# One-expert layers of an eight-expert transformer step: rows fetched by token instead of sent to slots, results stored by slot and fetched by token, norms cut finer

## The chip, the cores and the metric

One core of one Trainium2 chip runs the whole program. The metric is the device time in microseconds of one execution. Engines are TensorE (PE), VectorE (DVE), ScalarE (ACT), GpSimd (POOL) and SyncE (SP), which here only issues DMAs. Each has its own instruction stream; they meet at semaphores only.

## The reference

`x` is 4 x 1024 tokens of 128 numbers. Six residual steps are applied, each to the layer norm of `x`:

```
x = x + 0.5 * L0_ffn(norm(x))     # 8 experts, each token goes to one
x = x + L0_attn(norm(x))          # gated linear attention, a recurrence over the tokens, done in chunks
x = x + 0.5 * L0_ffn(norm(x))
x = x + 0.5 * L1_ffn(norm(x))     # 8 experts, each token goes to its best two
x = x + L1_attn(norm(x))          # gated attention unit
x = x + 0.5 * L1_ffn(norm(x))

def L0_ffn(x):                    # T = 4096 tokens, E = 8, cap = T // E
    probs = softmax(x @ Wg)
    # each expert takes its cap best tokens; a token goes to its best expert
    # among those that took it, or to its best expert if none did
    tok2exp = ...
    out[t] = probs[t, tok2exp[t]] * gelu(x[t] @ W1[e]) @ W2[e]
```

The matrices of `L0_ffn` are 128 x 256 and 256 x 128, those of `L1_ffn` 128 x 512 and 512 x 128.

## The kernel before

The 4096 tokens are 32 tiles of 128 rows; `x` and its norm `xn` stay in SBUF. The layers are called moe0, gla (the recurrent attention), moe2, moe3, gau (the gated unit) and moe6. moe0 and moe2 give each token one expert (K = 1), moe3 and moe6 two (K = 2).

**Experts.** `moe_vector` routes on VectorE: softmax, a search of 15 steps for the eight thresholds, and a slot number for each token so that the tokens of one expert stand together in tiles. Slots for K = 1 fill 39 tiles, 20 pairs. From the slot numbers TensorE inverts the list by one-hot matmuls into `token`, the token of each slot. The slot numbers are known at L865, `token` at L897 (K = 1, where L895 and L896 give empty slots rows of their own) or L900 (K = 2).

For K = 1 the rows travel so. `fill_sync` (SP) fills the DRAM array `xslots` with rows of `xn`. `slots_pool` (GpSimd) issues 32 indirect DMAs, L1080, one a tile of tokens, that send each row of `xn` to its slot. When all have landed, `slots_sync` (SP) fetches slots in order, four tiles an issue (L1021), into a ring of eight pairs. In the loop `finish` (VectorE, L942) copies the result of a pair from PSUM into a ring of four, `ysb`, once the scatter of four pairs earlier has landed; `slots_pool` sends the result by 39 indirect DMAs (L1089) to the row of its token. When all have landed, SP reads the results in token order into `yhome`.

For K = 2 `moe_pool` (GpSimd) gathers the rows from DRAM by `token` (L1065), one indirect DMA a tile, four pairs ahead of TensorE's transposes (`AHEAD`); `moe_sync` (SP) stores the results in slot order (L1040), and behind the loop `moe_bring` gathers them by slot number, one indirect DMA a tile (L1106), into a ring of 16 tiles.

**The loop over pairs.** TensorE runs in a fixed order: the transposes of pair t+3 (`turn`, L598 for K = 1, L603 for K = 2), the up-projection of t+2 (`up`, L619 to L621), the down-projection of t (`down`, L640 to L643). ScalarE takes the gelu (L694, L695), VectorE splits the turned rows (L921, L923) and the hidden ones (L931) into high and low bf16 halves, and copies the result.

**Combination and norm.** `combine` (VectorE, L983) adds gate times result to `x`, four tiles at a time, then the statistics of the next norm (L352). `moments` turns the statistics of a group of tiles into scale and shift, by some 20 small operations each of which waits for the one before (L321 to L332, and `newton`, L296 to L301). ScalarE then writes the norms (L403), TensorE turns four tiles a block (L379), VectorE (L367) or ScalarE (L413) copies them. Norm ln1 (ahead of gla) has groups of 8 and 24 tiles, and `halves`, a bf16 split of the turned norm (L370 on VectorE, L410 on ScalarE); ln2 (ahead of moe2) groups of 8, 8 and 16; ln3 (ahead of moe3) of 8 and 24. In `ln_tensor` the work on a turned block (router logits L391 or queries L1138) follows two blocks behind the turning. `moe_rows_pool` (GpSimd) splits the norm into halves for moe3's rows.

**gla.** 32 chunks of 128 tokens in four batches. TensorE in `stage2` multiplies an update of the state (L1175) once VectorE has subtracted (L1340) and scaled (L1343) the state before; ScalarE copies (L1231, L1232) two products, and behind them the chunk's output and its sum of squares (L1245, L1246). VectorE's scans (L1313) and reciprocals (L1319) serve four chunks each. After the last chunk `gla_vector` adds the result to `x` (L1380) and takes the statistics.

**Weights.** moe3's and moe6's weights are split into bf16 halves during moe0: the high ones on ScalarE, the low ones on VectorE (`split_low`, L258, eight operations of 128 x 1024) just ahead of moe0's loop.

## Time and profile before

| | us |
|---|---|
| median of 3 runs | 1283.04 (1280.93 to 1285.11) |
| the profiled execution | 1278.25 |
| its span, first to last instruction | 1276.1 |
| PE busy | 672.3 (53%) |
| DVE busy | 738.6 (58%) |
| ACT busy | 489.5 (38%) |
| POOL busy | 553.1 (43%) |

How to read it. Busy times are of one profiled execution; a difference is made against its own 1278.25, and the median is 4.8 above that. In a timeline a row gives the start in us, the duration (of several merged operations with xN), engine, line and operation, what it writes and reads, and in brackets how long the engine had been idle and what ended that. The duration of an indirect DMA on POOL is that of its issue, not of the transfer; the transfer's landing is seen at whoever waits for it. `<-remote` says that the releaser is nothing that the profile lists, such as a DMA's landing; `<-issue` that the engine waited for nothing that shows. The chain of work goes back from the last instruction, at each step to what released it.

### The profile page before, as it was taken

The numbers are of one execution on the slowest core, as the hardware profiler recorded it, in microseconds if no ns is written. First come the engines' busy times: TensorE is split into PE (matmuls) and PEld (weight loads), VectorE is DVE, ScalarE is ACT, GpSimd is POOL, SyncE is SP. The second block draws the span as 40 slices with busy tenths as digits, with TensorE's granted clock in tenths as the row PEclk, the third lists the DMA queues.
The fourth block names the chain that finished last, engine by engine and source line by source line (L and its number), as shares of the span: only waits on it lengthen the run. The fifth ranks groups of instructions, "written<-read, shape, count | busy, mean of one in ns | idle before, by whom it ended". The sixth has DMA issues, their size and how long they took to land.

```text
span 1276.1 us, 20751 instructions
## 1 busy us (share of the span) xinstructions
PE 672.3 (53%) x5982; PEld 544.7 (43%) x5983; DVE 738.6 (58%) x2301; ACT 489.5 (38%) x1079; POOL 553.1 (43%) x538
## 2 busy tenths in 40 slices
PE   4210582466646111870659999127777448999100
PEld 4210451245635000550648888014445337889100
DVE  6682354767884850547354556339985764556222
ACT  5300232544435000331507788126555206788000
POOL 2117563044440045561236666654311126663575
PEclk9999996679875555885558999668878659999655
DMA  9401313000000002213102334111000102335232
GB/s 294 120 8 46 92 57 92 1 1 0 0 3 1 1 27 80 72 43 90 50 23 68 76 82 67 49 43 34 25 17 9 34 15 67 77 81 71 61 82 68
DMA packets 86769, 67.78 MB, mean 53 GB/s; under 512 B 10522, under 2 KB 78362, under 8 KB 86706
## 3 DMA queue, kind: packets, MB, share of 16 engines
q1 hardware_dynamic: 72978, 38.99, 10.7%
q0 software_dynamic: 13728, 28.02, 9.4%
q8 instruction: 31, 0.51, 0.2%
q14 instruction: 32, 0.26, 0.1%
HBM read 38.53 MB, written 28.44 MB: 52 GB/s over the span
## 4 chain that ended last, share of the span: by engine, by line
PE 36%; DVE 26%; POOL 13%; issue 12%; ACT 6%; DMA 3%; another core or an unknown queue 3%; DVEq 0%; POOLq 0%; ACTq 0%; SPq 0%
POOL rt L1106 6%; POOL xslots L1080 5%; PE bank L619 4%; PE bank L640 4%; PE bank L621 3%; PE bank L643 3%; PE bank L620 3%; DVE rt L800 3%; PE bank L641 3%; PE bank L391 2%; DVE stats L352 2%; DVE x L983 2%; PE bank L603 1%; DVE turned L931 1%
## 5 line engine op out<-in xcount | busy, mean ns | idle before, releaser
L1065 POOL DMA_INDIRECT turned<-xrows_moe,token x156 | 168.7, 1081 | 144.1 <-DVE token L900 60.7
L702 ACT ACTIVATE turned<-bank,b1T 128x256 f32<-128x256 f32 x312 | 122.4, 475 | 111.4 <-PE bank L621 93.8
L1106 POOL DMA_INDIRECT rt<-y_moe,slot_i x128 | 122.7, 959 | 87.7 <-issue 37.2
L931 DVE TENSOR_TENSOR turned<-turned 128x1024 bf16<-128x1024 f32 (+1 forms) x118 | 125.3, 1062 | 34.9 <-ACT turned L706 18.5
L640 PE MATMUL bank<-w2h,turned 128*128 x780 | 141.0, 224 | 4.6 <-DVE turned L931 2.3
L641 PE MATMUL bank<-w2h,turned 128*128 x780 | 141.0, 224 | 1.0 <-issue 1.0
L619 PE MATMUL bank<-rt,w1h 128*128 128x256 bf16 (+1 forms) x468 | 126.3, 270 | 26.3 <-issue 11.1
L1080 POOL DMA_INDIRECT xslots<-xn,slot_i x64 | 69.4, 1084 | 163.1 <-DVE slot_i L865 144.2
L942 DVE COPY arena<-bank 128x256 f32<-128x256 f32 x118 | 49.8, 422 | 141.2 <-remote 89.9
L620 PE MATMUL bank<-rt,w1h 128*128 128x256 bf16 (+1 forms) x468 | 125.5, 268 | 0.0
L621 PE MATMUL bank<-rt,w1l 128*128 128x256 bf16 (+1 forms) x468 | 125.2, 268 | 0.0
L694 ACT ACTIVATE turned<-bank 128x512 f32<-128x512 f32 x40 | 23.9, 598 | 263.5 <-PE bank L621 229.1
L643 PE MATMUL bank<-w2l,turned 128*128 x780 | 122.9, 224 | 0.5 <-issue 0.4
L1089 POOL DMA_INDIRECT y_moe<-arena,token x78 | 77.8, 998 | 68.9 <-DVE arena L942 50.3
L379 PE MATMUL bank<-consts,xn 128*128 128x128 f32 x128 | 33.5, 412 | 115.7 <-ACT xn L403 115.6
L983 DVE SCALAR_TENSOR_TENSOR x<-rt,small,x 128x128 f32<-128x128 f32 x128 | 40.9, 349 | 77.2 <-DMA rt<-y_moe,slot_i 72.6
L640 PEld LDWEIGHTS bank<-w2h,turned 128*128 128x128 bf16 x780 | 76.8, 99 | 16.8 <-issue 10.8
L403 ACT ACTIVATE xn<-x,nwt 128x128 f32<-128x128 f32 x128 | 52.1, 482 | 82.3 <-DVE credit L360 81.9
L706 ACT ACTIVATE turned<-turned 128x1024 bf16<-128x1024 f32 x78 | 82.4, 1057 | 2.5
L641 PEld LDWEIGHTS bank<-w2h,turned 128*128 128x128 bf16 x780 | 77.8, 100 | 1.4 <-issue 0.9
L379 PEld LDWEIGHTS bank<-consts,xn 128*128 128x128 f32 x128 | 24.2, 226 | 124.0 <-ACT xn L403 90.0
L619 PEld LDWEIGHTS bank<-rt,w1h 128*128 x468 | 47.2, 101 | 51.8 <-issue 41.7
(302 smaller groups left out, 1835.4 us busy)
## 6 DMA issues: line engine op xcount, KB each, us to landing
y_moe<-arena SPq DMA_DIRECT2D x78, 128.0 KB
turned<-xslots SPq DMA_DIRECT2D x18, 256.0 KB
arena<-y_moe SPq DMA_DIRECT2D x16, 256.0 KB, 4.7
xslots<-xn SPq DMA_DIRECT2D x5, 512.0 KB, 6.0
turned<-xrows_moe,token POOLq DMA_INDIRECT x156
x<-in_x SPq DMA_DIRECT2D x4, 512.0 KB, 5.9
arena<-in_w SPq DMA_DIRECT2D x1, 2048.0 KB, 9.4
turned<-in_w SPq DMA_DIRECT2D x8, 256.0 KB, 4.4
```

The costliest lines, as they stand in the source:

```text
L619: nc.tensor.matmul(o, wh, xh_t, start=True, stop=False)
L620: nc.tensor.matmul(o, wh, xl_t, start=False, stop=False)
L621: last = nc.tensor.matmul(o, wl, xh_t, start=False, stop=True)
L640: nc.tensor.matmul(y[j], hh[j], wh, start=(u + j == 0 and not s["bias"]), stop=False)
L641: nc.tensor.matmul(y[j], hl[j], wh, start=False, stop=False)
L643: last = nc.tensor.matmul(y[j], hh[j], wl, start=False, stop=(u == FC - 1 and j == js[-1]))
L702: last = nc.scalar.activation(s["h32"][:, k % 2, o], bank[1 + 2 * (k % 2) + u // 2][:, W * (u % 2):W * (u % 2) + W], ACT.Gelu, bias=b1T[:, ...
L706: nc.scalar.activation(s["hh"][:, k % 4], s["h32"][:, k % 2], ACT.Copy).then_inc(s["act"], 1)
L931: nc.vector.tensor_tensor(s["hl16"][:, k % 4], s["h32"][:, r], s["hh"][:, k % 4], ALU.subtract)\
L1065: nc.gpsimd.indirect_dma_start(out=s["xs"][:, 2 * (t % BODY) + j], out_offset=None, in_=s["xdram"], in_offset=bass.IndirectOffsetOnAxis(ap ...
L1080: nc.gpsimd.indirect_dma_start(out=s["xdram"], out_offset=bass.IndirectOffsetOnAxis(ap=slot_i[:, 0, t:t + 1], axis=0), in_=xn[:, t, :], in ...
L1106: nc.gpsimd.indirect_dma_start(out=ytok[:, at % TOK], out_offset=None, in_=s["ydram"], in_offset=bass.IndirectOffsetOnAxis(ap=slot_i[:, k, ...
```

## The change

Seven parts.

1. For K = 1 rows and results travel as for K = 2: SP stores `xn` in token order (`rows_sync`), `moe_pool` gathers the rows by `token` four pairs ahead, `moe_sync` stores results by slot, `moe_bring_all` gathers them by slot number behind the loop. `fill_sync`, `slots_sync`, `slots_pool` and the rows of empty slots go.
2. `combine_all`: with K = 1 the statistics of a tile follow its addition at once, and after each addition three steps of the moments of the group before (`moments_by_steps`, a generator) are written out; the copies and splits of turned blocks follow two groups behind.
3. The groups: ln1 8, 8, 8, 4, 4; ln2 8, 8, 8, 8; ln3 8, 8, 8, 4, 4. In `gla_vector` the moments are written between additions and statistics.
4. The split of moe3's rows goes from GpSimd to ScalarE (high) and VectorE (low, `ln_rows`).
5. `ln_tensor`: logits and queries follow one block behind the turning.
6. `split_low` is halved: four operations ahead of moe0's loop, four behind it; the second weights are staged in `xn` and loaded once the rows are stored.
7. gla: the update matmul waits for the subtraction alone, the copy of the two products for a semaphore of its own, and the two copies are one; the sums of squares are copied once a batch.

```diff
         def load_w2(sp):
-            sp.wait_ge(pr["w0l"], 2)
+            sp.wait_ge(*ln0.at("turned", NS))
+            sp.wait_ge(*moe0.at("xrow", 16 * B))
...
+        def moments_by_steps(dve, s, g):
...
+            dve.wait_ge(*s.at("stat", b))
+            done(nc.vector.tensor_tensor(one(0), st(1), st(4), ALU.add))
+            yield
...
+        def some_steps(chain):
+            for _ in range(3):
+                next(chain, None)
...
+        def ln_halves(dve, s, blocks, chain=iter(())):
+            def copy(i):
...
+                dve.wait_ge(*s.at("turned", i + 1))
+                nc.vector.tensor_copy(xnT[:, o], bank[i % 2][:]).then_inc(s["copied"], 1)
+                next(chain, None)
+            def low(i):
...
+                dve.wait_ge(*s.at("copied", i + 1))
+                dve.wait_ge(*s.at("high", i + 1))
                 nc.vector.tensor_tensor(xl[:, o], xnT[:, o], xh[:, o], ALU.subtract).then_inc(s["low"], 1)
+                next(chain, None)
+            copy(blocks[0])
+            for i in blocks[1:]:
+                copy(i)
+                low(i - 1)
+            low(blocks[-1])
+        def ln_rows(dve, s, blocks, chain=iter(())):
+            for i in blocks:
+                tiles = slice(TPS * i, TPS * (i + 1))
+                dve.wait_ge(*s.at("high", i + 1))
+                nc.vector.tensor_tensor(xhl[:, tiles, P:2 * P], s["dst"][:, tiles], xhl[:, tiles, 0:P], ALU.subtract)\
+                    .then_inc(s["low"], 1)
+                next(chain, None)
...
-                if i >= 2:
-                    after(i - 2)
-            after(NS - 2)
+                if i >= 1:
+                    after(i - 1)
             return after(NS - 1)
...
+                if s["rows"]:
+                    tiles = slice(TPS * i, TPS * (i + 1))
+                    act.wait_ge(*s.at("norm", TPS * (i + 1)))
+                    nc.scalar.activation(xhl[:, tiles, 0:P], s["dst"][:, tiles], ACT.Identity).then_inc(s["high"], 1)
...
-                if K == 1:
-                    i = k % BODY // 2
-                    pe.wait_ge(fetched[i], FETCHED[s["layer"]][i] + 16 * (c + k // BODY) + 16)
-                else:
-                    pe.wait_ge(gathered[k % BODY], GATHERED[k % BODY][s["index"]] + 32 * (c + k // BODY) + 16 * len(js))
+                pe.wait_ge(gathered[k % BODY], GATHERED[k % BODY][s["index"]] + 32 * (c + k // BODY) + 16 * len(js))
...
-                if K == 1:
-                    dve.wait_ge(scattered[k % YRING], SCATTERED[k % YRING][s["index"]] + 32 * turns)
-                else:
-                    dve.wait_ge(ystored[k % YRING], YSTORED[k % YRING][s["index"]] + 16 * turns)
+                dve.wait_ge(ystored[k % YRING], YSTORED[k % YRING][s["index"]] + 16 * turns)
...
+                    if K == 1:
+                        some_steps(chain)
+                        dve.wait_ge(*s.at("comb", QUAD * quad + i + 1))
+                        next_stats([t])
...
+            for quad in range(groups[0][1] // QUAD):
+                combine(dve, s, quad, count)
+            for g in range(1, last + 1):
+                chain = moments_by_steps(dve, next_ln, g - 1)
+                for quad in range(groups[g][0] // QUAD, groups[g][1] // QUAD):
+                    combine(dve, s, quad, count, chain)
+                finish_steps(chain)
+                if 2 <= g < last:
+                    blocks(*groups[g - 2])
+            chain = moments_by_steps(dve, next_ln, last)
+            blocks(groups[last - 2][0], groups[last - 1][0], chain)
+            finish_steps(chain)
+            blocks(groups[last - 1][0], NT)
...
                     pe.wait_ge(gl["act1"], n + 3)
-                    pe.wait_ge(gl["state"], n + 1)
+                    pe.wait_ge(gl["dve"], n + 1)
                     nc.tensor.matmul(DS[:, 0:P], ga["kt"][:, i % 2], ga["v"][:, i % 2], start=True, stop=True)\
                         .then_inc(gl["update"], 1)
...
+                    pe.wait_ge(gl["state"], n + 1)
                     nc.tensor.matmul(O[:, 0:P], state, ga["qT"][:, tok], start=False, stop=True).then_inc(gl["st2"], 1)
...
-        ln1 = layernorm(x, xn, [8, 24], halves=True)
-        ln2 = layernorm(x, xn, [8, 8, 16])
+        ln1 = layernorm(x, xn, [8, 8, 8, 4, 4], halves=True)
+        ln2 = layernorm(x, xn, [8, 8, 8, 8])
...
-        ln3 = layernorm(x, xn, [8, 24])
+        ln3 = layernorm(x, xn, [8, 8, 8, 4, 4], halves="rows")
...
-            slots_pool(pool, moe0, gau_pool)
+            moe_pool(pool, moe0, gau_pool)
+            moe_bring_all(pool, moe0)
             gla_pool(pool)
             rows_pool(pool)
-            slots_pool(pool, moe2)
+            moe_pool(pool, moe2)
+            moe_bring_all(pool, moe2)
             gau_select(pool)
-            moe_rows_pool(pool, moe3)
...
-            moe_vector(dve, moe0, split_low)
+            moe_vector(dve, moe0, lambda dve: split_low(dve, 0), lambda dve: split_low(dve, 1))
```

## Rows read from the trace of the kernel before

**Rows 1.** The page, part 4: shares of the chain by line.
```profile
POOL rt L1106 6%; POOL xslots L1080 5%; PE bank L619 4%; PE bank L640 4%; PE bank L621 3%; PE bank L643 3%; PE bank L620 3%; DVE rt L800 3%; PE bank L641 3%; PE bank L391 2%; DVE stats L352 2%; DVE x L983 2%; PE bank L603 1%; DVE turned L931 1%
```
**Rows 2.** Timeline of POOL, first, one middle and last of moe0's scatters.
```profile
88.39 1.91 POOL L1080 DMA_INDIRECT xslots<-xn,slot_i  x1 [52.27 <-DVE slot_i L865]
...
100.69 1.96 POOL L1080 DMA_INDIRECT xslots<-xn,slot_i  x1 [0.30 <-issue]
...
133.20 0.97 POOL L1080 DMA_INDIRECT xslots<-xn,slot_i  x1 [0.30 <-issue]
```
**Rows 3.** Chain in moe0, timeline of PE in moe2: first up-projection of each.
```profile
140.23 0.28 PE bank L619
...
507.82 0.29 PE L619 MATMUL bank<-rt,w1h 128*128 128x128 bf16 x1 [0.77 <-DVE rt L923]
```
**Rows 4.** Timeline of DVE ahead of moe0's loop, and of moe2's.
```profile
94.36 0.23 DVE L895 TENSOR_SCALAR rt<-iotas,consts 128x40 f32<-128x40 f16 x1
...
96.05 4.63 DVE L258 TENSOR_TENSOR w1l<-arena,w1h 128x1024 bf16<-128x1024 f32 x4
...
139.12 0.42 DVE L921 CAST rt<-bank 128x256 bf16<-128x256 f32 x1 [33.91 <-PE bank L598]
...
465.25 0.23 DVE L895 TENSOR_SCALAR rt<-iotas,consts 128x40 f32<-128x40 f16 x1
```
**Rows 5.** Waits of DVE over the span, and its last result copies in moe0.
```profile
DVE arena L942 <- remote: 89.9, 49, 4.0
...
206.05 0.76 DVE L942 COPY arena<-bank 128x256 f32<-128x256 f32 x2 [4.02 <-remote]
```
**Rows 6.** Timelines around ln1 and ln3: DVE moments (first, last), ACT, PE, DVE.
```profile
219.06 0.17 DVE L321 TENSOR_TENSOR nwt<-stats 128x8 f32<-128x8 f32 x1
...
222.19 0.17 DVE L332 TENSOR_TENSOR nwt<-nwt 128x8 f32<-128x8 f32 x1
...
238.38 1.63 ACT L403 ACTIVATE xn<-x,nwt 128x128 f32<-128x128 f32 x4
...
257.87 1.85 PE L1152 MATMUL bank<-turned,wkT_s 128*128 128x512 f32 x2 [0.89 <-ACT arena L1211]
...
627.10 0.42 DVE L771 TENSOR_REDUCE small<-bank 128x32 f32<-128x256 f32 x1 [18.98 <-PE bank L391]
```
**Rows 7.** Timelines of DVE, POOL and PE where moe3's loop starts.
```profile
653.10 0.24 DVE L900 TENSOR_SCALAR token<-bank 128x78 int32<-128x78 f32 x1 [0.87 <-PE bank L562]
...
654.14 1.27 POOL L1065 DMA_INDIRECT turned<-xrows_moe,token  x1 [31.50 <-DVE token L900]
...
661.81 0.39 PE L619 MATMUL bank<-rt,w1h 128*128 128x256 bf16 x1 [0.33 <-issue]
```
**Rows 8.** PE's transposes in moe2's loop; a window (PE, PEld, DVE, ACT, POOL, clock, DMA).
```profile
521.46 0.41 PE L598 MATMUL bank<-consts,turned 128*128 128x128 f32 x2
...
524.08 0.41 PE L598 MATMUL bank<-consts,turned 128*128 128x128 f32 x2
...
503.00:510.00 7.00, 3.26 (x23) 2.69 (x24) 1.60 (x4) 0.49 (x1) 0.00 (x0) 0.50 0.65 187
```
**Rows 9.** Timeline of DVE behind moe6's loop: last copy, first and last use.
```profile
1185.71 0.42 DVE L942 COPY arena<-bank 128x256 f32<-128x256 f32 x1 [1.57 <-PE bank L643]
...
1191.41 0.35 DVE L983 SCALAR_TENSOR_TENSOR x<-rt,small,x 128x128 f32<-128x128 f32 x1 [5.27 <-DMA rt<-y_moe,slot_i]
...
1270.68 0.35 DVE L983 SCALAR_TENSOR_TENSOR x<-rt,small,x 128x128 f32<-128x128 f32 x1 [0.90 <-DMA rt<-y_moe,slot_i]
```
**Rows 10.** Timeline of PE in gla: the update matmul and what it waited for.
```profile
314.12 0.46 PE L1175 MATMUL bank<-arena 128*128 128x128 f32 x2 [1.97 <-DVE arena L1343]
```
**Rows 11.** Timeline of DVE: moe2's router takes its first reduction.
```profile
409.87 0.42 DVE L771 TENSOR_REDUCE small<-bank 128x32 f32<-128x256 f32 x1 [14.39 <-PE bank L391]
```
**Rows 12.** Timeline of DVE in gau's first steps, while POOL gathers (L1106).
```profile
830.20 0.17 DVE L1745 TENSOR_TENSOR nwt<-stats 128x4 f32<-128x4 f32 x1 [3.72 <-issue]
...
833.70 0.17 DVE L1750 TENSOR_SCALAR nwt<-nwt 128x4 f32<-128x4 f32 x1 [3.18 <-remote]
```

268 lines of the change are left out of this document (124 added, 144 removed).

## The prediction

> **What bounds the kernel now.** I read the page's chain of work first [rows 1]: no engine is the bound throughout, and the two dearest lines of the chain are not arithmetic but GpSimd's indirect DMAs, L1106 (results fetched by token for the two-expert layers) with 6% and L1080 (rows sent to their slots for the one-expert layers) with 5%. Then I cut the span at the stages by the timelines of single engines. In the first one-expert layer VectorE knows the slots at 88 us, GpSimd issues 32 scatters one behind the other, the last at 133.20 [rows 2], and TensorE's first up-projection starts at 140.23 [rows 3]; VectorE has stood 33.91 us before it [rows 4]. Then 20 pairs of tiles run until 206.4 [rows 5], and the combination, the norm and the queries until the keys' matmul at 257.87 [rows 6]. The second one-expert layer is the same 370 us later: first up-projection 507.82, next router's first reduction 627.10 [rows 3, 6]. Inside the loops the longest wait is VectorE's copy of results, 89.9 us in 49 waits for something outside the engines [rows 5]: a ring buffer that comes free only when the result scatter of four pairs earlier has landed. So three things bound these layers: 32 exposed issues ahead of the loop, a scatter in the loop, and a norm of 24 tiles that can't start before its last tile.
>
> **Issues are exchanged, not removed.** Per one-expert layer GpSimd had 32 scatters ahead of the loop and 39 in it; now it has 39 gathers in the loop and 32 behind it. What was exposed ahead of the loop is exposed behind it. The gain must come from what can run beside the 32, from a faster loop, and from fewer landings in series. I therefore sum each layer from end to end, from the moment the token list is known.
>
> **First layer.** The token write takes the place of the operation at 94.36 [rows 4], since what stood before it is dropped. In the two-expert layer, which has the same gathers, the token write at 653.10, the first gather at 654.14 and the first up-projection at 661.81 give 1.0 and 7.7 us [rows 7] (up-projection 0 waits for the rows of pair 1, four issues). Four instead of eight of the weight splits now run on VectorE just there; beside them an issue took 1.96 instead of 0.97 us [rows 2]. Up to three of the four issues are hit; I take 1.5 us, between 0 and 3. 94.4 + 1.0 + 7.7 + 1.5 = 104.6 for the first up-projection, instead of 140.2.
> The Trainium skill, page "SBUF — State Buffer", section "Who interferes with whom", says that a tensor_tensor without a two-port mode should not hold up the writing of descriptors; by it these 1.5 us, and 1 more below, would be 0. The issue at 100.69 beside the split says otherwise.
>
> The loop: two transposes in a row of TensorE start at 521.46 and 524.08 with nothing missing between them, so TensorE needs 2.62 us a pair at full clock [rows 8]. GpSimd's two issues need 2 x (0.97 + 0.30) = 2.54 us [rows 2]. The result store moves to SP, and its ring no longer waits for GpSimd. The two rates are nearly equal and coupled by a ring four pairs deep: at least 20 x 2.62 = 52.4, and I add 5.6 for filling, draining and jolts: 58.0, against 66.2 now. Bounds: 55 (perfect) and 66 (as now). At the low clock, with which the second layer starts (0.50 [rows 8]), TensorE is a little over 3 us a pair at first; 1 us there. Last result copy 162.6.
>
> Behind it: in the last layer the last result copy starts at 1185.71, the first use of a gathered tile at 1191.41, the 64th at 1270.68 [rows 9]: 5.7 us, and 79.27 / 63 = 1.258 us a tile. For 32 tiles 39.0 us. The other four weight splits (4.6 us [rows 4]) fit into the 5.7 but slow two issues: 1 us. First use 169.3, last tile landed 208.3.
>
> Beside the gathers VectorE now does combination, statistics, three steps of the moments a tile and the norm's copies. One tile: 0.27 + 0.2 for the two operations and some 0.43 for three dependent steps (20 steps take 3.1 us when bare [rows 6]), 0.9 us. This alone would keep up with 1.258. But each pair of blocks adds two copies and two subtractions (four of 0.69, 2.8 us, by what each takes at 128 x 512) and a hole: ScalarE writes the next block's four norms (1.63 [rows 6]) between the two halves VectorE waits for. I take 4.5 us a pair of blocks. Followed through in order, from the first use: groups 0 and 1 are paced by the gathers until 20; group 2 ends at 30, its blocks at 34.3; group 3 at 39, blocks at 43.9; the last four tiles at 48.6; then blocks 4 and 5 with the last steps, 56, where the last tile landed at 39. Then norms 1.6, turning 1.1, a copy, two query matmuls and their activations, some 7.5: 64. So the keys' matmul at 169.3 + 64 = 233.3 against 257.87: **24.6 us gained**. A check: today the way from the last statistics' end, 233.5, to the keys is 24.4 us with nothing hidden; put behind the last landing it would be 39 + 24.4 = 63.4. By my count the finer norm thus gives nothing that VectorE's fixed order doesn't take back.
>
> **Second layer.** Token write 465.25 [rows 4], nothing else on VectorE: 465.3 + 1.0 + 7.7 = 474.0. Loop 59 (with the clock), then 5.7: 538.7. The tail is the same with cheaper blocks (3.5, since ScalarE copies and VectorE only subtracts) and norms, turning and two blocks of logits, 5.8, at the end: 58.5. 597.2 against 627.10: **29.9 gained**. GpSimd's split of rows for the next layer goes to ScalarE and VectorE; I count it in these blocks. Its store to memory lies below the routing, over 25 us long.
>
> **The recurrent layer.** TensorE's update matmul now waits for the difference, not for the scaled state, so it runs beside the 0.35 us scaling; where it waited 1.97 us for L1343 it now waits 0.4 less [rows 10]. Its 0.46 us also stood on the chain. ScalarE merges two copies and leaves out seven of eight small ones. VectorE's scans and reciprocals, some 10 of 24 us a batch, stay. 32 chunks, a third of them waiting so: 32 x 0.46 / 3 = 5. Bounds 0 (VectorE bound throughout) and 12. **5 us.** The norm behind it: four groups of eight with moments between the additions, last group 8 instead of 16 tiles. Today four blocks of TensorE follow the last moments, the router's reduction waiting 14.39 us to 409.87 [rows 11]. New: the last moments end at about 393.6, only 1 us earlier, but the blocks 4 and 5 are turned before; two blocks remain: 402.8. **7 us**, between 4 and 8. The first norm turns logits one block earlier; TensorE is the bound there, 0 within 1 us either way. The second weights' load moves behind the rows' store on SP, into the norm's buffer; its cover is the routing, until 88 us [rows 2], and if it were late ScalarE would only start its splits later beside the gathers: 0. The row stores that open the one-expert layers lie there too. SP's 20 result stores a layer stand behind nothing else on its queue. Routing, both two-expert layers and the gating layer: 0.
>
> **Sum.** 24.6 + 29.9 + 5 + 7 = 66.5. The profiled execution took 1278.25 (2.1 around its span of 1276.1): 1211.8. The median of the runs stands 4.8 above it, 1283.04: **1217 us**, the forecast.
>
> **Rivals.**
> B. VectorE keeps up. If ScalarE's halves come early and steps hide beside other work, the last norms start soon after the last tile: 39 + 8 for the last steps + 7.5 = 54.5 to the keys, 39 + 7.2 + 5.8 = 52 to the router. That is 9.5 and 6.5 us less, and 3 more each with the loops at 55: 22, about 1195. For it: the bare step's 0.2 us is latency, its issue takes under 0.1. Against it: four engines in fixed orders must meet in each block.
> C. Loops no faster than now, and stalls. VectorE stood 3.72 us before L1745, then twice 3.2 more, and ran its next steps at some 0.7 instead of 0.2 us, while GpSimd gathered [rows 12]; about 16 us in all, in code that runs once. The new combination is such code beside such gathers. With loops at 66 (+8 each) and 8 us of stall a layer left on the path: 66.5 - 32 = 34.5, about 1249; one of the two alone gives 1233. For it: [rows 12], and that the loop's rate has two makers of equal speed; against it: the quads before and after show no such stall.
> The Trainium skill, page "Runtime: NRT & Kernel Launch", section "Instruction fetch mechanics", says that passing to the next block of instructions is mostly hidden in straight code. If the waits of [rows 12] are that, the rows differ from it by 3 us each; what they are no row tells.
> D. Slower than before. The same stall in every quad of the new combination: there are 16 in the two layers, and from 66.5 / 16 = 4.2 us a quad on the gain is gone. Stalls of 3.72 and some slow steps, 6 us a quad, would give 1217 + 96 = 1313. Against it: the gating layer has eight quads and stood so in one or two.
> That the change doesn't do what it says, in its finer norms, is the check above: it costs nothing against the forecast.
>
> **Chances.** Forecast 0.50, B 0.25, C 0.20, D 0.05, of which 0.02 at about its point of balance. The range takes in B and C: 1194 to 1249. Faster by over 0.3% (about what a measurement of this kernel can tell from no change) 0.95, within 0.02, slower 0.03.
>
> **What the profile of after would show.** GpSimd's first gather of the first layer at 95 to 96, first up-projection at 104 to 106 (right if within 2 us); pairs at 2.7 to 2.9 us, and the copy's waits for something outside near 0; 32 gathers 1.26 us apart; VectorE's last combination some 9 us behind the last landing; keys near 233, the router's reduction after the second one-expert layer near 561 (627.1 less 66.5). It is wrong if pairs take over 3.1 us (C), if VectorE waits for a landing at the last tile (B), or if VectorE shows repeated idle times of 3 us in the combination (C, D).

## The result, and the profile after

| | before | after |
|---|---|---|
| median, us | 1283.48 (1280.93 to 1285.11, 4 runs) | 1260.88 (1259.44 to 1265.05, 4 runs) |
| ratio after / before | | 0.983 (95%: 0.980 to 0.985) |
| the profiled execution / its span | 1278.25 / 1276.1 | 1261.09 / 1257.9 |

The change gained 22.6 us by the medians (of four runs each here, of three in the table ahead of the prediction) and 17.2 between the two profiled executions, where the forecast was 66.5. The time is 44 us above the forecast and outside the range. The stations of the prediction, in the changed kernel (timelines of GpSimd, TensorE and VectorE; columns as in the rows ahead of the prediction):

```profile
93.32 1.11 POOL L1104 DMA_INDIRECT turned<-xrows_moe,token  x1 [57.12 <-DVE token L956]
...
101.95 0.29 PE L684 MATMUL bank<-rt,w1h 128*128 128x128 bf16 x1 [0.47 <-issue]
...
169.08 0.42 DVE L994 COPY arena<-bank 128x256 f32<-128x256 f32 x1 [0.43 <-PE bank L708]
...
175.40 0.35 DVE L1033 SCALAR_TENSOR_TENSOR x<-rt,small,x 128x128 f32<-128x128 f32 x1 [1.35 <-DMA rt<-y_moe,slot_i]
...
253.94 1.10 PE L1171 MATMUL bank<-turned,wkT_s 128*128 128x512 f32 x2 [0.89 <-ACT arena L1231]
...
361.07 2.19 DVE L1401 SCALAR_TENSOR_TENSOR x<-xn,nwt,x 128x128 f32<-128x128 f32 x8
...
395.13 0.42 DVE L836 TENSOR_REDUCE small<-bank 128x32 f32<-128x256 f32 x1 [9.33 <-PE bank L472]
...
458.71 0.29 PE L684 MATMUL bank<-rt,w1h 128*128 128x128 bf16 x1 [0.25 <-issue]
...
526.54 0.42 DVE L994 COPY arena<-bank 128x256 f32<-128x256 f32 x1 [0.32 <-PE bank L708]
...
532.55 0.35 DVE L1033 SCALAR_TENSOR_TENSOR x<-rt,small,x 128x128 f32<-128x128 f32 x1 [5.58 <-DMA rt<-y_moe,slot_i]
...
606.55 0.42 DVE L836 TENSOR_REDUCE small<-bank 128x32 f32<-128x256 f32 x1 [0.64 <-PE bank L472]
```

Set beside [rows 3, 6, 11]: the first up-projection comes 38.3 us earlier, but gla's keys only 3.9; the router behind gla 14.7; the router behind moe2 20.6. So nearly all the gain of the front was given back behind it. That the 32 gathers now stand behind the loop was forecast; two stretches of each one-expert layer took longer than that. The first is the loop: first up-projection to last result copy is 67.1 us in moe0 and 67.8 in moe2, where 58 and 59 were forecast and the kernel before took 66.2 and 63.5. The second is the tail, from the first addition to the keys, 78.5 us, and in moe2 to the router, 74.0, where 64 and 58.5 were forecast.

What each place shows. Where the loop begins, ScalarE and VectorE stand 7 to 9 us (their timelines), and over the run the result copy waits as before for something outside the engines (waits of VectorE: total, times, longest):

```profile
113.85 0.60 ACT L759 ACTIVATE turned<-bank 128x512 f32<-128x512 f32 x1 [8.94 <-remote]
...
114.00 0.42 DVE L976 CAST rt<-bank 128x256 bf16<-128x256 f32 x1 [7.57 <-remote]
```

```profile
DVE arena L994 <- remote: 94.6, 65, 3.0
...
DVE arena L994 <- PE bank L708: 37.1, 38, 2.0
```

This total is of all four expert layers, as the 89.9 us of [rows 5] are. In moe0's and moe2's loops alone the copy stood 13.0 and 14.8 us so (9 and 11 times), and 66.9 us in moe3's and moe6's.

In the tail VectorE keeps up with the gathers until 193 us; then this (timeline of VectorE):

```profile
193.12 0.16 DVE L402 TENSOR_TENSOR nwt<-nwt 128x8 f32<-128x8 f32 x1
194.59 0.29 DVE L352 BATCH_NORM_STATS2 stats<-x 128x6 f32<-128x128 f32 x1 [1.31 <-issue]
...
197.41 0.29 DVE L352 BATCH_NORM_STATS2 stats<-x 128x6 f32<-128x128 f32 x1 [2.28 <-remote]
197.62 0.34 DVE L1033 SCALAR_TENSOR_TENSOR x<-rt,small,x 128x128 f32<-128x128 f32 x1
...
205.14 0.17 DVE L376 TENSOR_SCALAR nwt<-nwt 128x8 f32<-128x8 f32 x1 [2.99 <-remote]
205.22 0.16 DVE L378 SCALAR_TENSOR_TENSOR nwt<-nwt 128x8 f32<-128x8 f32 x1
205.30 0.22 DVE L380 TENSOR_SCALAR nwt<-nwt 128x8 f32<-128x8 f32 x1
207.94 0.29 DVE L352 BATCH_NORM_STATS2 stats<-x 128x6 f32<-128x128 f32 x1 [2.42 <-remote]
208.15 0.34 DVE L1033 SCALAR_TENSOR_TENSOR x<-rt,small,x 128x128 f32<-128x128 f32 x1
211.45 0.17 DVE L383 TENSOR_TENSOR nwt<-nwt 128x8 f32<-128x8 f32 x1 [2.96 <-issue]
215.64 0.17 DVE L386 TENSOR_SCALAR nwt<-nwt 128x8 int32<-128x8 int32 x1 [4.02 <-remote]
```

Read it by what each instruction waits for. L352, L376, L383 and L386 (and L369, at 199.51, not shown) wait for a semaphore that VectorE itself has just incremented, and start 1.3 to 4.0 us late. L378 and L380 wait for nothing, and L1033 waits for a tile that has long landed: they start at once. Eight such starts from 193 to 216 are 19.3 us (1.31 + 2.28 + 1.55 + 1.76 + 2.99 + 2.42 + 2.96 + 4.02). They end with the gathers: the last long one begins at 211.62, when the last gather is issued (211.57), and two of 0.5 to 0.6 us follow. moe2's tail shows eight more between 553 and 573, 0.9 to 3.7 us each, 18.3 us together. I call them late starts.

### The profile page after: what moved, and what is told of

It reads as the page before. It is cut to its first block, busy times and chain, and to the rows that moved or that the text cites. A ratio compares the mean times of both kernels' runs of the same rounds, so it can differ in the third digit from the quotient of the medians.

```text
span 1257.9 us, 20818 instructions
## 1 busy us (share of the span) xinstructions
PE 679.3 (54%) x5975; PEld 545.5 (43%) x5983; DVE 759.4 (60%) x2446; ACT 489.1 (39%) x1027; POOL 530.8 (42%) x530
## 4 chain that ended last, share of the span: by engine, by line
PE 35%; DVE 21%; issue 12%; POOL 9%; ACT 6%; another core or an unknown queue 4%; DMA 2%; POOLq 0%; DVEq 0%; ACTq 0%
POOL rt L1124 8%; PE bank L684 4%; PE bank L705 4%; PE bank L686 3%; PE bank L685 3%; PE bank L706 3%; PE bank L708 3%; DVE rt L865 2%; PE bank L668 1%; ACT xn L484 1%; DVE x L1033 1%; DVE stats L352 1%; DVE arena L1339 1%; POOL turned L1104 1%
## 5 line engine op out<-in xcount | busy, mean ns | idle before, releaser
L1104 POOL DMA_INDIRECT turned<-xrows_moe,token x234 | 243.4, 1040 | 373.4 <-DVE token L956 243.2
L1124 POOL DMA_INDIRECT rt<-y_moe,slot_i x192 | 183.5, 956 | 139.4 <-DMA y_moe<-arena 57.6
L994 DVE COPY arena<-bank 128x256 f32<-128x256 f32 x118 | 50.0, 424 | 131.9 <-remote 94.6
L1033 DVE SCALAR_TENSOR_TENSOR x<-rt,small,x 128x128 f32<-128x128 f32 x192 | 63.0, 348 | 96.2 <-DMA rt<-y_moe,slot_i 91.9
L708 PEld LDWEIGHTS bank<-w2l,turned 128*128 128x128 bf16 x780 | 64.1, 99 | 4.4 <-issue 3.9
L686 PEld LDWEIGHTS bank<-rt,w1l 128*128 x468 | 48.1, 103 | 5.6 <-issue 0.6
```

The source lines that it names most:

```text
L686: last = nc.tensor.matmul(o, wl, xh_t, start=False, stop=True)
L708: last = nc.tensor.matmul(y[j], hh[j], wl, start=False, stop=(u == FC - 1 and j == js[-1]))
L1033: nc.vector.scalar_tensor_tensor(x[:, t, :], ytok[:, at % TOK], gates[k][:, t:t + 1], x[:, t, :], ALU.mult, ALU.add).then_inc(s["comb" if ...
L1104: nc.gpsimd.indirect_dma_start(out=s["xs"][:, 2 * (t % BODY) + j], out_offset=None, in_=s["xdram"], in_offset=bass.IndirectOffsetOnAxis(ap ...
L1124: nc.gpsimd.indirect_dma_start(out=ytok[:, at % TOK], out_offset=None, in_=s["ydram"], in_offset=bass.IndirectOffsetOnAxis(ap=slot_i[:, k, ...
```

## The experiments

"Beside it" is the kernel before on the same chip; a ratio is against it, with its 95% interval. The eighteen kernels ran in five sets on five chips. The chip turned out to matter more than most edits, so I take the sets in the order in which they ran.

**Transport by SP in the tail.** The results are then those of other tokens, and only time and waits are read.

```diff
+            for at, t in enumerate(s["order"]):
+                if at >= 6:
+                    sp.wait_ge(*s.at("comb", at - 5))
+                sp.dma_start(ytok[:, at % TOK], s["ydram"][P * t:P * (t + 1)]).then_inc(direct[at % 6], 16)
...
-            moe_bring_all(pool, moe0)
```

> Edit: in moe0 and moe2 the 32 tiles of results behind the loop are fetched by SP with plain DMAs in slot order instead of by GpSimd's indirect gathers by slot number (results are then those of other tokens: the order by token is left out). Same bytes, same VectorE code. Theory S (VectorE gets its code late while GpSimd's gathers are in flight): the idle times of 1.3 to 4.0 us in VectorE's combination (22 us in moe0, 20 in moe2) are gone, each below 0.6 us; with the tiles arriving faster too, the keys' matmul of gla at 253.9 comes 20 to 35 us earlier. Rival W (the code itself, its waits from step to step or for ScalarE and TensorE, makes these times): they stay, some 20 us in each layer, wherever the tiles come from.

1189.64 us, beside it 1277.78. From the first addition at 172.46 the keys come in 49.9 us:

```profile
222.37 1.10 PE L1183 MATMUL bank<-turned,wkT_s 128*128 128x512 f32 x2 [0.89 <-ACT arena L1243]
```

No late start is left in the tails; the long waits of VectorE in moe0's are six for ScalarE, 5.5 us, and one of 2.1 for TensorE, and the changed kernel has these too (5.5 and 2.0). The same VectorE code without GpSimd's gathers beside it is not late. W is out. (The loops still gather, and keep their 65.9 and 66.2 us.)

**More code, a larger ring, a closer lead.** Three kernels on the same chip.

```diff
+            for i in range(64 * s["index"], 64 * s["index"] + 64):
+                nc.vector.memset(padding[:, i:i + 1], 0.0)
```

> Edit: 64 tiny VectorE memsets stand ahead of the combination of moe0 and of moe2, where VectorE waits 5.6 us for the first gathered tile anyway. Theory S (VectorE lives on a stock of instructions and its refill is slow while GpSimd gathers): the stock is used up 64 instructions earlier, so the first idle time over 1.3 us comes some 9 tiles earlier in the code, near 10 to 14 us behind the first gather instead of 21, and the sum of these times grows by 8 to 20 us a layer. Rival A (the stalls depend on how long the gathers have been running): first long idle time again 21 to 24 us behind the first gather (194.6 and 553.8 in their own run), sum as before, time within 5 us.

1254.92 us. The late starts did not come earlier but later: the first one's idle time begins at 195.7, 25 us behind the first gather at 170.82 (21 in the changed kernel), and it stands some 64 + 10 instructions further on in the code. Their sum did not grow either: 17.8 us in moe0's tail, where the changed kernel's is 20.4 (both counted from 0.5 us up). Rival A comes nearest. So a stock of instructions that runs out is not what makes them, and the same is said by which instructions are late. The Trainium skill, page "Runtime: NRT & Kernel Launch", section "Instruction fetch mechanics", has it that fetching is mostly hidden in straight code; the run agrees as far as it goes, and theory S in the form tested here fell.

```diff
-        YRING = 4
+        YRING = 8
```

> Edit: the ring of result buffers holds 8 pairs instead of 4, in all four expert layers. Theory R (the result copy waits until the store of four pairs earlier has landed, beside the gathers): its waits for something outside the engines (94.6 us in 65 waits) fall below 20, moe0's loop from 66 to 60 us, moe2's likewise, moe3's and moe6's pairs from 3.3 towards 3.0 us, in all 15 to 40 us faster. Rival E (the pair's period is set by TensorE and GpSimd, the copy's wait only takes up their slack): the waits go to other lines, time within 4 us.

1254.83 us, ratio 0.979 (0.973 to 0.985), not told apart from the changed kernel's own ratios (0.983 above, 0.982 and 0.980 below), and the same time as the padded kernel's on this chip. The waits did not go:

```profile
DVE arena L994 <- remote: 80.0, 57, 2.9
```

The padded kernel, with the ring of four and on the same chip, has 72.7 us of them. In moe0's and moe2's loops they are 8.8 and 9.9 us with the ring of eight, 9.2 and 7.7 with the ring of four. In moe0's first eight pairs no place of this ring has been used before, and yet four copies stood 1.5 to 2.3 us there. The ring is not what the copy waits for. That was my reading of [rows 5].

```diff
-                    if at >= TOK:
+        LOOK = 4
...
+                    if K == 1 and at >= LOOK:
+                        pool.wait_ge(*s.at("comb", at - LOOK + 1))
+                    elif at >= TOK:
```

> Edit: in moe0 and moe2 GpSimd brings tile n only once VectorE has combined tile n-4 (instead of n-16), so gathers pause when VectorE falls behind. Theory S: the pauses let VectorE's code come in, so its long idle times shrink from about 20 us a layer to 5 to 10; 10 to 25 us faster in all. Rival W (the stalls have nothing to do with gathers in flight): they stay and the gathers end later too, 0 to 15 us slower.

1230.20 us, ratio 0.961 (0.955 to 0.967): 2 per cent below the changed kernel's ratio, and 24.6 us below the padded kernel and the one with the larger ring. The tails are 66.0 and 63.6 us. GpSimd runs at 1.25 us a tile for 21 tiles, late starts begin as ever, VectorE falls behind, and now GpSimd must stop:

```profile
198.12 0.17 DVE L377 TENSOR_SCALAR nwt<-nwt 128x8 f32<-128x8 f32 x1 [2.94 <-remote]
```

```profile
199.09 0.94 POOL L1127 DMA_INDIRECT rt<-y_moe,slot_i  x1 [3.28 <-remote]
```

After this pause, 11 more gathers pass (with another pause, of 1.77 us, among them) without one late start above 0.5 us. In moe2 pauses of 1.25 and 2.57 us do nearly the same (late starts of 1.6 us at most follow). The changed kernel, whose GpSimd may be 16 tiles ahead, never pauses.

**Waits, increments, more lead: another chip.** I then looked for what gathers do to VectorE's semaphores.

```diff
-                    if at >= TOK:
+                    if at >= TOK and K == 2:
...
-                        out=ytok[:, at % TOK], out_offset=None, in_=s["ydram"],
+                        out=ywide[:, at] if K == 1 else ytok[:, at % TOK], out_offset=None, in_=s["ydram"],
```

> Edit: in moe0 and moe2 the 32 brought tiles have a buffer each (not a ring of 16), so GpSimd's gathers behind the loop wait for nothing of VectorE's; two tiles share a semaphore, and VectorE waits for both. VectorE's code is the same otherwise. In the changed kernel the long idle times begin at 193 and 552, just where GpSimd issues its 17th gather, the first that stands behind a wait for VectorE's additions; each of them stands before an instruction that waits for one of VectorE's own semaphores, and while they last VectorE's increments come through at one per 1.2 to 1.3 us, the pace of the gathers. Theory G (a GpSimd that is busy with gathers and has such waits between them lets VectorE's increments through only one per gather): the idle times vanish, each below 1 us, 15 to 20 us less in each layer, 30 to 40 us faster in all. Theory S (code comes late beside gathers) and theory M (increments come late beside gathers in general): they stay from about the same place, time within 5 us of the changed kernel.

> Edit: as the run with a buffer for each tile, but GpSimd's waits for VectorE's additions stand again before gathers 17 to 32, though nothing needs them. Theory G: the idle times are back from the 17th gather on, about 20 us a layer. Theories S and M: the same as with a buffer for each tile, whatever that shows.

```diff
-            done(nc.vector.tensor_tensor(one(1), st(1), st(4), ALU.subtract))
+            done(nc.vector.tensor_tensor(one(1), st(1), st(4), ALU.subtract), 0)
...
-            done(nc.vector.tensor_tensor(one(2), st(2), st(5), ALU.add))
+            done(nc.vector.tensor_tensor(one(2), st(2), st(5), ALU.add), 3)
```

> Edit: the changed kernel with the same VectorE instructions and waits, but fewer semaphore increments: the steps of the moments that nobody waits for one by one, and the statistics of all but a group's last tile, increment nothing (the last one of them increments by the whole number). Some 2.7 instead of 5 increments a tile. Theory G or M (late increments, about one per gather): the idle times start at the same place, and their sum falls from 22 and 20 us to about half; 15 to 25 us faster in all. Theory S: sum unchanged, time within 5 us.

```diff
-                if t >= AHEAD:
-                    pool.wait_ge(*s.at("turned", t - AHEAD + 1))
+                if t >= BODY:
+                    pool.wait_ge(*s.at("turned", t - BODY + 1))
```

> Edit: in all four expert layers the rows of a pair are gathered as soon as their place in the ring of eight pairs is free (eight pairs ahead instead of four). Theory L (the loop's rate suffers from gathers that start late behind TensorE's turning, GpSimd and the result copy both held until the same moment): pairs from 3.2 to 2.7 us, moe0's loop 60 instead of 66 us, 15 to 40 us faster. Rival E (the pair's period is made elsewhere, the gathers are early enough): pairs as before, time within 5 us; the gathers crowd together at the loop's start, where DVE and ACT stood 7 to 9 us, and this may grow.

All four take nearly the same: 1172.97, 1170.91, 1168.24 and 1168.78 us, and beside them the kernel before took 1224.80 instead of 1278. The three ratios are 0.954 to 0.958, each within 0.005. All four lack late starts, the needless waits' run too, and the unedited kernel before is some 53 us faster as well, so the edits are hardly the reason. The run with eight pairs ahead has the tails of the changed kernel unchanged; its waits, stations and the place of the late starts:

```profile
DVE arena L994 <- PE bank L708: 68.3, 110, 2.8
```

```profile
101.56 0.29 PE L684 MATMUL bank<-rt,w1h 128*128 128x128 bf16 x1 [0.45 <-issue]
...
161.03 0.42 DVE L994 COPY arena<-bank 128x256 f32<-128x256 f32 x1 [0.43 <-PE bank L708]
...
167.26 0.36 DVE L1033 SCALAR_TENSOR_TENSOR x<-rt,small,x 128x128 f32<-128x128 f32 x1 [1.27 <-DMA rt<-y_moe,slot_i]
...
201.68 0.16 DVE L376 TENSOR_SCALAR nwt<-nwt 128x8 f32<-128x8 f32 x1
...
202.55 0.17 DVE L386 TENSOR_SCALAR nwt<-nwt 128x8 int32<-128x8 int32 x1
...
229.96 1.10 PE L1171 MATMUL bank<-turned,wkT_s 128*128 128x512 f32 x2 [0.89 <-ACT arena L1231]
...
559.58 0.42 DVE L836 TENSOR_REDUCE small<-bank 128x32 f32<-128x256 f32 x1 [0.64 <-PE bank L472]
```

The wait for something outside the engines is gone from the list altogether. The loop takes 59.5 us and the tail 62.7 (moe2: 59.7 and 58.3). The three others, whose loops are the changed kernel's word for word, take 59.3 to 60.3 us for them, so the longer lead is not what shortened the loop.

**Controls.** The next set held the changed kernel, the kernel before, and two of the four again.

> No edit: the changed kernel itself, as the control for this chip. In the four runs with a buffer for each tile, with needless waits, with fewer increments and with eight pairs ahead, no long idle time of the kind in question was left at all, in no stage, and the kernel before ran 4% faster than in its own run: so these four say nothing of the edits if the chip is what differs. Theory V (whether VectorE's and TensorE's increments arrive late beside gathers is a property of the chip, and the first two sets of runs met chips that have it): where the kernel before takes near 1225 the changed kernel shows no such idle times and takes 1165 to 1175, some 55 us less; where it takes near 1280 the changed kernel takes 1255 to 1262 and has idle times of 1.3 to 4 us from the 17th gather behind the loop on. Rival (the edits did it): near 1200 beside 1225, with those idle times.

> No edit: the kernel before, for its trace on this chip. Theory V: where it takes near 1225, its result copy's waits for something outside the engines (89.9 us in 49 waits in its own run) are nearly all gone too, though it has the same ring of four result buffers and the same scatters. Rival (those waits are for the landing of the scatter of four pairs earlier): they stay above 60 us on every chip.

> Edit: the kernel with a buffer for each brought tile and no waits of GpSimd behind the loop, again. On a chip with late increments, theory G: no idle time over 1 us in VectorE's combination, 30 to 40 us less than the control. Theories M and S: idle times as in the control, time within 6 us of it. On a chip without: within 5 us of the control.

> Edit: the kernel with fewer semaphore increments (2.7 instead of 5 a tile in the combination), again. On a chip with late increments, theory G or M: idle times from the same place, sum about half, 15 to 25 us less than the control. Theory S: as the control. On a chip without: within 5 us of the control.

This chip has late starts. The changed kernel took 1264.23 us (ratio 0.982, 0.975 to 0.988), the kernel before 1283.06 with its copy's waits at

```profile
DVE arena L942 <- remote: 74.9, 44, 3.2
```

the run with a buffer for each tile 1261.60, that with fewer increments 1261.23 (ratio 0.982, 0.975 to 0.989). Theory V's half for a chip with late starts came true. G falls, and so does M's forecast that fewer increments halve the sum: it is 20.4 us in moe0's tail and 19.4 in moe2's (from 0.5 us up), where the changed kernel has 18.9 and 17.6 here. The kernel before was not traced on a chip without late starts, so whether its copy's waits vanish there is not shown. Late starts of the one with a buffer for each tile and no waits of GpSimd, then of the one with fewer increments:

```profile
205.47 0.43 DVE L376 TENSOR_SCALAR nwt<-nwt 128x8 f32<-128x8 f32 x1 [2.96 <-remote]
...
211.78 0.17 DVE L383 TENSOR_TENSOR nwt<-nwt 128x8 f32<-128x8 f32 x1 [2.96 <-remote]
215.97 0.17 DVE L386 TENSOR_SCALAR nwt<-nwt 128x8 int32<-128x8 int32 x1 [4.02 <-remote]
```

```profile
202.97 0.17 DVE L380 TENSOR_SCALAR nwt<-nwt 128x8 f32<-128x8 f32 x1 [3.01 <-issue]
...
209.27 0.17 DVE L387 TENSOR_TENSOR nwt<-nwt 128x8 f32<-128x8 f32 x1 [2.96 <-issue]
213.47 0.17 DVE L390 TENSOR_SCALAR nwt<-nwt 128x8 int32<-128x8 int32 x1 [4.03 <-remote]
```

The same instructions (in the second, four lines further on) are late by the same times as in the changed kernel. Neither the waits nor the increments set them. Theory S would fit these two as well, but the padding and the choice of the late instructions speak against it.

**Old norm, ticks, rows by SP.** A further chip with late starts; the changed kernel as the control.

> No edit: the changed kernel, the control for this chip. If the kernel before takes near 1280: 1255 to 1265, with idle times of 1.3 to 4 us in the tails. If near 1225: 1165 to 1175, none of them.

1261.72 us, ratio 0.980 (0.976 to 0.985).

```diff
-        ln1 = layernorm(x, xn, [8, 8, 8, 4, 4], halves=True)
+        ln1 = layernorm(x, xn, [8, 24], halves=True)
...
+            for quad in range(NT // QUAD):
+                combine(dve, s, quad, count)
+                for g, (a, b) in enumerate(groups):
+                    if b == QUAD * (quad + 1):
+                        ln_moments(dve, next_ln, g)
+                        if g:
+                            blocks(*groups[g - 1])
+            blocks(*groups[-1])
```

> Edit: the norms behind the one-expert layers undone to what they were (groups of 8 and 24, additions in fours and then their statistics, the moments whole at the end of a group, all turned blocks' work at the end), the transport of the change kept. The prediction counted 63.4 us from the first addition to the keys' matmul this way against 64 with the finer norm. Theory N (the finer norm gives nothing on a chip without late starts, and costs much on one with them, since it puts 60 dependent steps beside the gathers): without late starts within 6 us of the control; with them 20 to 35 us faster than the control. Rival O (the finer norm is worth its way even so, since it hides three of five groups): 10 to 25 us slower than the control.

1245.24 us, ratio 0.968 (0.963 to 0.972): 16.5 below the control. The tails are 68.6 and 68.0 us instead of 79.2 and 74.0. So on such a chip the finer norm costs 16.5 us, in N's direction and somewhat less than its 20 to 35: it puts dependent steps of the moments beside the gathers, which the old norm does behind them, but the old norm's statistics wait for VectorE's additions too and are late as well.

```diff
+                    if K == 1:
+                        tick(at + NT * s["index"])
```

> Edit: in moe0 and moe2 a small GpSimd memset (128 x 16) stands before each gather behind the loop, so gathers come some 0.2 us further apart; nothing else waits for it. With gathers held four tiles ahead of VectorE (spaced 1.43 us on average) the late starts had shrunk from 21 to about 4 us a layer. Theory D (gathers without a pause make VectorE's results known late; a short pause in each is enough): late starts below 6 us a layer, 25 us faster than the control on a chip that has them. Rival K (what helped was that VectorE and GpSimd waited for each other): late starts as in the control, 0 to 12 us slower. On a chip without late starts: 5 to 12 us slower.

1261.69 us, late starts as in the control. But it tested no pause: the memset went into the gap of 0.3 us, and the gathers came 1.25 to 1.26 us apart as before (timeline of GpSimd).

```profile
208.28 0.95 POOL L1131 DMA_INDIRECT rt<-y_moe,slot_i  x1 [0.18 <-issue]
209.23 0.12 POOL L1116 MEMSET ticks<- 128x16 f32 x1
209.54 0.95 POOL L1131 DMA_INDIRECT rt<-y_moe,slot_i  x1 [0.18 <-issue]
```

```diff
+                sp.dma_start(s["xs"][:, 2 * (t % BODY):2 * (t % BODY) + 2], tiles[:, a:a + 2]).then_inc(direct[t % AHEAD], 16)
...
-            for t in range(s["pairs"]):
+            for t in range(s["pairs"] if s["K"] == 2 else 0):
```

> Edit: in moe0's and moe2's loops the rows of a pair are fetched by SP with plain DMAs in token order (the order by slots is left out, so the results are those of other rows); the start still waits for the token list, four pairs ahead as before; the gathers behind the loop stay. Theory B (the loop's lost time comes from GpSimd's gathers beside it): VectorE's 7.6 us and ScalarE's 8.9 us waits where the loop begins fall below 3, the result copy's waits for something outside vanish, moe0's loop takes 56 to 59 instead of 66 us. Rival C (the loop's code or the result stores make it): the waits stay, 64 to 67 us. On a chip without late starts: loops as in the control within 3 us.

1254.33 us. The waits went as B said: in moe0's loop, and in moe2's, neither VectorE nor ScalarE waits for anything outside the engines any more, with the ring of four and the same stores. The result copy's 62.5 us of such waits that are left over the run all lie in moe3 and moe6, which still gather. The time did not: first up-projection 102.87, last copy 168.92, 66.1 us. TensorE now waited for the new fetches, which SP issues behind the result stores (waits of TensorE in the loop, then of VectorE):

```profile
PE bank L667 <- DMA turned<-xrows_moe: 7.0, 8, 1.3
```

```profile
DVE arena L998 <- PE bank L712: 20.4, 19, 2.0
DVE rt L980 <- PE bank L667: 7.1, 8, 1.3
```

So waits of this kind need the gathers. How much of the loop's time is theirs the run doesn't show, since another wait took their place.

**Pauses.**

```diff
+                    if K == 1 and at % 12 == 0 and at:
+                        pool.wait_ge(*s.at("comb", at))
+                    elif at >= TOK:
```

> Edit: the changed kernel, but in moe0 and moe2 GpSimd brings tile 13 only once VectorE has combined the first 12, and tile 25 once it has combined 24; each of these two waits makes a pause of some 2.5 us for the landing and the addition. Theory D (late starts build up over some 16 gathers that follow each other without a pause, and a pause of 2 to 3 us clears them), on a chip that has late starts: none above 1.2 us in the tails, from the first addition to gla's keys 65 to 69 us instead of 79, from the first addition of moe2 to the router's reduction 61 to 65 instead of 74, in all 18 to 28 us less than the changed kernel's 1261, near 1237. Rival K (only being held close to VectorE all the time helps): late starts come back behind the first pause, 1255 to 1265. On a chip without late starts: 4 to 10 us slower than 1169.

> Edit: the same two pauses, and the norms behind the one-expert layers undone to groups of 8 and 24 with whole moments at a group's end, as in the run of the old norm. The prediction counted the finer norm at nothing (64 against 63.4 us from the first addition to the keys). If that holds once late starts are away, this is within 6 us of the run with the pauses alone, on any chip. Rival (the finer norm is worth what its three hidden groups save): 10 us or more slower than the run with the pauses alone.

This set met a chip without late starts (beside it 1228.07). The pauses: 1175.48 us, ratio 0.957 (0.951 to 0.962). With the old norm: 1182.09 us, ratio 0.963 (0.958 to 0.969). Keys and router of the first, then of the second:

```profile
232.62 2.05 PE L1173 MATMUL bank<-turned,wkT_s 128*128 128x512 f32 x2 [0.88 <-ACT arena L1233]
...
566.75 0.42 DVE L836 TENSOR_REDUCE small<-bank 128x32 f32<-128x256 f32 x1 [0.64 <-PE bank L472]
```

```profile
235.45 1.10 PE L1164 MATMUL bank<-turned,wkT_s 128*128 128x512 f32 x2 [0.89 <-ACT arena L1224]
...
572.82 0.42 DVE L836 TENSOR_REDUCE small<-bank 128x32 f32<-128x256 f32 x1 [0.65 <-PE bank L472]
```

From the first additions (167.41 and 505.02; 167.64 and 506.18) these are tails of 65.2 and 61.7 us, with the old norm 67.8 and 66.6. The finer norm is worth 2.6 and 4.9 us here, 6.6 by the medians, whose ranges overlap (1172.7 to 1180.1 and 1177.8 to 1184.3): a little more than the 6 expected, and less than the rival's 10. Whether pauses alone keep late starts away stays untested, since there were none to keep away.

## Why the prediction was wrong, point by point

What occurred is rival C, with both of its halves: loops no faster than before and stalls beside the gathers. Both of its signs showed, result copies 3.2 us apart (120.20, 123.37, 126.60) and repeated idle times of 3 us. It was priced at 1249 and the kernel took 1260.88.

The terms, as the prediction summed them, on a chip with late starts (the changed kernel's own run) and on one without (the kernel with eight pairs ahead, whose lead in the loops is its only difference):

| | forecast | with late starts | without |
|---|---|---|---|
| moe0: token known to first up-projection | 10.2 | 9.7 | 9.6 |
| moe0: first up-projection to last copy | 58.0 | 67.1 | 59.5 |
| moe0: last copy to first addition | 6.7 | 6.3 | 6.2 |
| moe0: first addition to keys | 64 | 78.5 | 62.7 |
| moe2: first up-projection to last copy | 59 | 67.8 | 59.7 |
| moe2: first addition to router | 58.5 | 74.0 | 58.3 |
| gla: keys to first addition (was 111.5) | 106.5 | 107.1 | 107.9 |
| ln2: first addition to router (was 40.5) | 33.5 | 34.1 | 34.1 |

(In the first row the token list is written at 92.27 with late starts and at 91.93 without. gla's first addition behind the recurrence stood at 369.37 before, and ln2's two terms are measured from it.)

**The front was nearly right.** First gather at 93.3 (I said 95 to 96), first up-projection at 101.95 (104.6). That is 2.7 us early, just outside the 104 to 106 that I gave, and 2.1 of it is the token list, written at 92.27 and not at 94.4. Three gathers were issued beside the splits (93.65 to 98.3); one took 1.95 us, as the issue of [rows 2] did, the two others 1.11 and 0.97, which is what later ones take. The Trainium skill, page "SBUF — State Buffer", section "Who interferes with whom", infers that a tensor_tensor leaves the writing of descriptors alone, and says beside it that one with both inputs in SBUF, as these splits are, contends with what GpSimd reads. I took only the first half; the trace has one issue of three slowed by 1 us.

**gla and ln2 were right**: 4.4 us for the 5 forecast, 6.4 for the 7.

**The step that failed is "its ring no longer waits for GpSimd".** I read the 89.9 us of [rows 5] as the ring of results waiting for a scatter's landing, and took them for removed. The trace of before already spoke against that. Its waits of VectorE in moe0's loop, moe2's, moe3's and moe6's:

```profile
DVE arena L942 <- remote: 19.8, 7, 4.0
...
DVE arena L942 <- remote: 19.4, 8, 3.1
...
DVE arena L942 <- remote: 26.5, 17, 3.0
...
DVE arena L942 <- remote: 24.1, 17, 1.5
```

More than half of them, 50.6 us, lie in moe3 and moe6, where no result is scattered and the change changes nothing. The changed kernel has 94.6 us of such waits with stores from SP, 27.8 of them in the two loops that it changed. A ring twice as large still has 80.0. In the runs on chips without late starts there are none, and none in a loop without gathers (where the rows come by SP). So they go with the gathers and with the kind of chip, as the late starts do, and I take them for the loop's form of them; that is an inference from where they appear. The loops took 9.1 and 8.8 us longer than forecast. Without late starts they take 59.3 to 60.3 us in all six runs. TensorE's clock is not what makes this difference: on average it was granted 1.00 of full speed in moe0's loop of the second control, which took 66.6 us, and 0.94 in the needless waits' run, which took 59.4.

**The second is the 0.9 us a tile and 4.5 a pair of blocks taken for the whole tail.** Rival C named it: straight code beside gathers, 3 us a time, seen in [rows 12]. I priced it at 8 us a layer; with 19.3 and 18.3 us of late starts in them the tails took 14.5 and 15.5 us longer than forecast. The price was about half of what it should have been, and its reason was wrong too: I looked for code that comes late, where the rows say which instructions are late. L1745 and L1750 of [rows 12] are instructions that wait for VectorE's own results as well, and L1746, L1747, L1751 and L1752 between them, which wait for nothing, followed at 0.08 us in that trace. I read the length of their idle times and not what they had in common.

The sum of the failures: (9.1 + 14.5 - 2.7 for the earlier start) + (8.8 + 15.5) = 45.2, for 45.9 missing at the router behind moe2 (66.5 forecast there, 20.6 found). Some 2 us more went in moe3 and gau. Rivals B (1195) and D (1313) did not occur; D's stall in every quad is bounded by the gathers' end.

**Where the chip has no late starts the forecast's stations held**: keys at 230.0 against 233.3, router behind moe2 at 559.6 against 561. The forecast of the time would not have: the 1168.78 us there are 48 below 1217, and outside the range on the other side. The reason is the stretch behind moe2's router, which the prediction carried over from the old trace as 649.0 us; the changed kernel took 651.4 for it, and the one with eight pairs ahead 609.1 without late starts. So the prediction took the untouched layers with their late starts, as the old trace had them, and the changed layers without. The gain there is 56.0 us (1224.80 to 1168.78, with eight pairs ahead), not 66.5, since the kernel before is itself faster by some 58 us: it seems to pay for late starts too. Where in it they lie is not shown, since it was not traced on such a chip. The changed kernel itself was not run on such a chip. Going from one kind of chip to the other costs the kernel before some 58 us (1283 to 1225) and the changed one some 92 (1261 to 1169, by the kernel with eight pairs ahead). The difference of 34 us is the gain that was lost.

**The check on the norm** said 63.4 with the old norm for 64 with the finer one. Without late starts the finer norm is worth 2.6 and 4.9 us, with them it costs 10.6 and 6.0 (g1's tails against the control's). "Gives nothing" was right to 3 us in moe0 and hid that its price depends on what runs beside it.

**What stays open.** Why some chips have late starts, and what in the gathers makes them. Each chip was met in one set only, so whether it is the chip itself or its state at that time can't be told either. What is shown: they need GpSimd's gathers beside them; they hit instructions that wait for what another instruction has just finished; in the tail their idle times begin 21 to 27 us after the first gather, and the long ones are over within 6 us of the last gather's issue; they depend neither on 64 more instructions ahead of them nor on how many increments there are. That a pause clears them is seen once in each layer of one run, and was not tested by a run of its own.

## What to carry to other kernels

A wait for something outside the engines is not evidence for the ring or the landing that would be the natural reason: before counting it as removed, look at who else stood until the same moment, at which instructions are late and which are not, and at whether stages without that ring or landing show it too. Keep dependent small steps of one engine out of the time in which GpSimd issues gathers without a pause, or hold the gathers only a few tiles ahead of their use: on such chips a lead of 4 instead of 16 tiles was worth 2 per cent and cost nothing in code (how it does on a chip without late starts was not run). Compare kernels on the same chip, and put the unchanged one beside them each time: the same program differed by 4 to 5% between chips, more than the 1.7% of the change.

## What the hardware showed unexpectedly

- The kernel before took 1224.80 and 1228.07 us on two chips and 1277.78 to 1287.30 on three others (medians of seven runs each), at nearly the same granted clock: 0.782 to 0.797 on the two, 0.772 to 0.791 on the three.
- On the chips with late starts VectorE starts instructions that wait for its own last result up to 4.0 us late in the tails of the changed kernel (4.6 in gau, 5.3 with the old norm), while instructions between them that wait for nothing follow at 0.08 us. The starts lie on a grid: 194.59, 197.41, 199.51, 201.61, 205.14, 207.94, 211.45, 215.64 are 4, 3, 3, 5, 4, 5 and 6 times 0.70 us apart. What has this period no row tells.
- In the loops on such a chip GpSimd's next gather starts 0.27 to 0.28 us behind the result copy again and again (120.20 and 120.48, 123.37 and 123.64, 126.60 and 126.88): both stood until the same moment, though the gather waits for TensorE's transposes and the copy for its down-projection.
- A GpSimd memset of 128 x 16 (0.12 us) between two gathers costs almost no time: their distance is 1.25 to 1.26 us, against 1.25 without it.
